# Twelve row one-hot slots in place of eight, and the mix's product, sum and spill taken up later in the step loop of a graph layer

## What is computed

```python
xn = layernorm(x)                              # x: 6250 x 256, f32
# two graph layers over 200,000 edges (src, dst); src uniform, dst = 6250 * u**2 with u uniform
agg = segment_sum(h[dst], src); h = silu(norm((h + agg / deg) @ W.T + b) * g + beta)
# a linear attention mix, 8 heads of 64: dots = k.T v (k, v normalised), out = q dots / N
mix = (q @ dots / N) @ w_out.T + b_out
x = x + gnn(xn) + mix
x = x + moe_ffn(layernorm(x))                  # 2 of 8 experts, layer norm after
```

## Time and profile before

| | |
|---|---|
| median of 3 runs | 3315.58 us (3312.92 to 3317.39) |
| profiled execution, its own time | 3316.68 us |
| its span, first to last instruction | 3314.9 us |
| step loop in it | about 666 to 1742 us |
| PE busy | 2628.7 us (79%) |
| DVE busy | 2009.6 us (61%) |
| ACT busy | 1309.2 us (39%) |
| mean granted PE clock | 0.924 of full speed |

### The profile page before, as it was taken

The page is one execution under the profiler, slowest core; times in us unless marked ns, Lnnn a source line. Parts: engine busy times, 40 slices in busy tenths (PEclk is TensorE's granted clock), DMA queues, the critical chain, the costliest instruction groups (busy, mean ns, idle before and its releaser), DMA issues. The chain is left out here.

```text
span 3314.9 us, 54424 instructions
## 1 busy us (share of the span) xinstructions
PE 2628.7 (79%) x16782; PEld 1850.4 (56%) x16782; DVE 2009.6 (61%) x4822; ACT 1309.2 (39%) x2213; POOL 169.5 (5%) x160
## 2 busy tenths in 40 slices
PE   0666555575858888877768999999799999986997
PEld 0333343332324444443327888888688888864665
DVE  8878899989888888889961222222122222236555
ACT  0333212244646666667691222222222221225666
POOL 0000000000000000000000000000011111114000
PEclk9888768687989999999969999999899999997999
DMA  5000000013213223223324444444544444410000
GB/s 159 0 0 1 0 0 0 10 45 132 104 56 127 104 91 117 98 95 121 121 81 155 150 148 150 143 147 151 182 137 138 138 130 137 138 60 29 26 25 27
DMA packets 153846, 304.75 MB, mean 92 GB/s; under 512 B 28963, under 2 KB 125476, under 8 KB 153700
## 3 DMA queue, kind: packets, MB, share of 16 engines
q1 hardware_dynamic: 101796, 217.44, 20.7%
q10 hardware_dynamic: 51776, 85.24, 7.0%
q0 software_dynamic: 128, 0.26, 0.0%
HBM read 196.54 MB, written 106.37 MB: 91 GB/s over the span
## 5 line engine op out<-in xcount | busy, mean ns | idle before, releaser
L1046 PE MATMUL banks<-ring 128*128 128x512 f16 x1650 | 517.2, 425 | 256.7 <-DVE ring L1652 126.8
L1076 PE MATMUL banks<-outer,ring 128*128 128x257 f16 x2450 | 543.9, 274 | 15.6 <-DMA outer<-table,heavy 8.6
L743 ACT ACTIVATE ring<-banks 128x512 f16<-128x512 f32 x637 | 382.2, 600 | 433.3 <-POOLq L604 431.4
L1076 PE MATMUL banks<-tabs,ring 128*128 128x257 f16 x2450 | 542.4, 274 | 8.6 <-DMA ring<-counts 8.6
L1077 PE MATMUL banks<-outer,ring 128*128 128x256 f16 x2450 | 543.7, 273 | 0.0
L1077 PE MATMUL banks<-tabs,ring 128*128 128x256 f16 x2450 | 542.3, 273 | 0.0
L1652 DVE TENSOR_SCALAR ring<-val,outer 128x512 f16<-128x512 f16 x1650 | 473.4, 348 | 78.5 <-PE banks L1046 77.4
L1046 PEld LDWEIGHTS banks<-ring 128*128 128x128 f16 x1650 | 230.7, 146 | 512.8 <-issue 450.9
L744 ACT ACTIVATE banks<-banks 128x512 f32<-128x512 f32 x637 | 383.5, 602 | 0.0
L1076 PEld LDWEIGHTS banks<-outer,ring 128*128 128x128 f16 x2450 | 238.7, 97 | 49.0 <-DMA outer<-table,heavy 8.9
L1076 PEld LDWEIGHTS banks<-tabs,ring 128*128 128x128 f16 x2450 | 238.4, 97 | 41.9 <-issue 9.5
(11 more groups left out here) (337 smaller groups left out, 3012.2 us busy)
## 6 DMA issues: line engine op xcount, KB each, us to landing
ring<-counts SPq DMA_DIRECT2D x98, 800.0 KB, 4.7
counts<-ring ACTq DMA_DIRECT2D x84, 896.0 KB, 3.9
ring<-counts SPq DMA_DIRECT2D x98, 768.0 KB, 4.1
tabs<-in_fw SPq DMA_DIRECT2D x4, 2048.0 KB, 9.0
outer<-in_x SPq DMA_DIRECT2D x5, 1280.0 KB, 13.4
outer<-in_x SPq DMA_DIRECT2D x25, 256.0 KB, 2.8
residual<-outer SPq DMA_DIRECT2D x25, 256.0 KB, 2.1
table<-tabs SPq DMA_DIRECT2D x25, 256.0 KB, 2.5
```

The lines of the kernel that those rows point to most:

```text
L743: act.activation(held[:, b, :, c, :], cell_bank.rearrange("p (q r) -> p q r", r=P), ACT.Copy, scale=0.25).then_inc(s_cell, 1)
L1046: mm(ps[:, bass.ds(at, 512)], hot_c[:, t // 8 % 2, :, t % 8], hot_r[t % RSLOTS], start=False, stop=False, skip_group_check=True).then_inc( ...
L1076: mm(o[:, 0:D + 1], a, xtab[l][:, cb, D:2 * D + 1], start=cb == 0, stop=False)
```

## The change

- `RSLOTS` goes from 8 to 12. The four new slots lie in unused columns of `outer` (one) and `big` (three). The wait ahead of a group becomes "all but the last eight steps done".
- The output product is issued one tile at a time: tile 0 behind group n + 6, tile 1 behind n + 7, each with its own `s_op`. The copy to `xT` stands ahead of group n + 5, the sum ahead of n + 12, the spill ahead of gate n + 14, the x rows ahead of gate n + 18.
- The transposes of pair p wait for the copy of pair p - 1 (`s_oxT`); the sum of pair p - 1 is now waited for by the product.
- M and G products, their copies and the run facts stand six groups apart in place of four; `HEAVY_AT` 22 becomes 26, `WMAX_AT` 48 becomes 60, the first weight load is 26 groups behind `HEAVY_AT`, and `piece_rows` comes two groups later.

```diff
--- before.py
+++ after.py
@@ -59,7 +59,7 @@
 PB = [0, 128, 512, 1024, 1536, 2048, STEPS]
 CW = 7
 NBK = 4
-RSLOTS = 8
+RSLOTS = 12
 IOTA = 640
 
 assert W * P >= P * EC and RB <= 49 and G + 1 < 1 << 10 and NCB % CW == 0 and G < IOTA
@@ -90,7 +90,7 @@
 
 
 
-M_AT, HEAVY_AT, WMAX_AT, SCALES_AT = 2, 22, 48, 132
+M_AT, HEAVY_AT, WMAX_AT, SCALES_AT = 2, 26, 60, 132
 OUT_AT = {**{140 + 8 * i: i for i in range(10)}, **{260 + 8 * i: 10 + i for i in range(11)},
           **{388 + 8 * i: 21 + i for i in range(4)}}
 TABLE_AT = {424 + 5 * i: i for i in range(NP)}
@@ -99,10 +99,10 @@
 assert len(OUT_AT) == len(TABLE_AT) == NP and max(TABLE_AT) + 2 < NG
 
 
-SPILL_AT = {n + 9: p for n, p in OUT_AT.items()}
-XIN_AT = {n + 13: p + 2 for n, p in OUT_AT.items() if p + 2 < NP}
+SPILL_AT = {n + 14: p for n, p in OUT_AT.items()}
+XIN_AT = {n + 18: p + 2 for n, p in OUT_AT.items() if p + 2 < NP}
 WRITE_AT = {n + 2: p for n, p in TABLE_AT.items()}
-WLOAD_AT = {HEAVY_AT + 18: 0, **{WMAX_AT + 10 * k + 2: k + 1 for k in range(4)}}
+WLOAD_AT = {HEAVY_AT + 26: 0, **{WMAX_AT + 10 * k + 2: k + 1 for k in range(4)}}
 
 REST_AT = 200
 
@@ -247,6 +247,7 @@
         hot_c = ringf[:, 0:1024].bitcast(F16).rearrange("p (b c k) -> p b c k", b=2, k=8)
         hot_r = [ringf[:, 1024 + n * 256:1280 + n * 256].bitcast(F16) for n in range(6)]
         hot_r += [outer[:, 9152 + n * 256:9408 + n * 256].bitcast(F16) for n in range(2)]
+        hot_r += [outer[:, 12096:12352].bitcast(F16)] + [big[:, 3328 + n * 256:3584 + n * 256].bitcast(F16) for n in range(3)]
         held = ringf[:, 2560:6144].bitcast(F16).rearrange("p (b q c r) -> p b q c r", b=2, q=GR // P, r=P)
 
 
@@ -1008,17 +1009,18 @@
                     pe.wait_ge(s_sc, 3)
                     pe.wait_ge(s_w, 16 * 11)
                 else:
-                    pe.wait_ge(s_oa, p)
+                    pe.wait_ge(s_oxT, p)
                 transposes(xn[:, p * 2 * D:(p + 1) * 2 * D], bank[4]).then_inc(s_otp, 1)
 
-            def out_product(p):
-                pe.wait_ge(s_oxT, p + 1)
-                for q in range(2):
-                    for c in range(DC):
-                        mm(bank[6][:, q * D:(q + 1) * D], xT[p % 2][:, (q * DC + c) * P:(q * DC + c + 1) * P],
-                           g_s[:, c * D:(c + 1) * D], start=c == 0, stop=False)
-                    m = mm(bank[6][:, q * D:(q + 1) * D], ones[0:1, :], borow, start=False, stop=True)
-                m.then_inc(s_op, 1)
+            def out_product(p, q):
+                if q == 0:
+                    pe.wait_ge(s_oxT, p + 1)
+                    if p:
+                        pe.wait_ge(s_oa, p)
+                for c in range(DC):
+                    mm(bank[6][:, q * D:(q + 1) * D], xT[p % 2][:, (q * DC + c) * P:(q * DC + c + 1) * P],
+                       g_s[:, c * D:(c + 1) * D], start=c == 0, stop=False)
+                mm(bank[6][:, q * D:(q + 1) * D], ones[0:1, :], borow, start=False, stop=True).then_inc(s_op, 1)
 
             def banks_of_steps(at):
 
@@ -1052,18 +1054,19 @@
                             pe.wait_ge(s_ready, piece)
                             pe.wait_ge(s_oa, sum(o < n for o in OUT_AT))
                         piece_part(piece, n - first_n - 1)
-                if n in (M_AT, M_AT + 4):
-                    m_products((n - M_AT) // 4)
-                if n == M_AT + 8:
+                if n in (M_AT, M_AT + 6):
+                    m_products((n - M_AT) // 6)
+                if n == M_AT + 12:
                     g_products()
-                if n in (HEAVY_AT + 1, HEAVY_AT + 5, HEAVY_AT + 9, HEAVY_AT + 13):
-                    run_turn((n - HEAVY_AT) // 4)
+                if n in (HEAVY_AT + 1, HEAVY_AT + 7, HEAVY_AT + 13, HEAVY_AT + 19):
+                    run_turn((n - HEAVY_AT) // 6)
                 if n == SCALES_AT - 1:
                     weight_scales()
                 if n in OUT_AT:
                     out_transposes(OUT_AT[n])
-                if n - 4 in OUT_AT:
-                    out_product(OUT_AT[n - 4])
+                for q_out in range(2):
+                    if n - 6 - q_out in OUT_AT:
+                        out_product(OUT_AT[n - 6 - q_out], q_out)
             pe.wait_ge(s_free, NBK + G)
             pe.wait_ge(s_oa, NP)
 
@@ -1597,7 +1600,7 @@
                 dve.tensor_copy(xT[p % 2][:, :], bank[4]).then_inc(s_oxT, 1)
 
             def mixed(p):
-                dve.wait_ge(s_op, p + 1)
+                dve.wait_ge(s_op, 2 * p + 2)
                 dve.wait_ge(s_xin[p % 2], 16 * (p // 2 + 1))
                 dve.tensor_tensor(xin[p % 2], xin[p % 2], bank[6], op=ALU.add).then_inc(s_oa, 1)
 
@@ -1614,24 +1617,24 @@
                 for first_n, piece in PIECE_AT.items():
                     if 0 <= n - first_n <= CH:
                         chunks_past(piece, n - first_n)
-                    if n == first_n + CH + 5:
+                    if n == first_n + CH + 7:
                         piece_rows(piece)
                 if n == M_AT - 1:
                     dots_diagonal()
-                if n in (M_AT + 3, M_AT + 7):
-                    m_copy((n - M_AT) // 4)
-                if n == M_AT + 11:
+                if n in (M_AT + 5, M_AT + 11):
+                    m_copy((n - M_AT) // 6)
+                if n == M_AT + 17:
                     g_copy()
-                if n >= HEAVY_AT and (n - HEAVY_AT) % 4 == 0 and n <= HEAVY_AT + 16:
-                    runs((n - HEAVY_AT) // 4)
+                if n >= HEAVY_AT and (n - HEAVY_AT) % 6 == 0 and n <= HEAVY_AT + 24:
+                    runs((n - HEAVY_AT) // 6)
                 if n >= WMAX_AT and (n - WMAX_AT) % 10 == 0 and n < WMAX_AT + 40:
                     weights_max((n - WMAX_AT) // 10)
                 if n == SCALES_AT:
                     weight_scales()
-                if n - 3 in OUT_AT:
-                    mixed_xT(OUT_AT[n - 3])
-                if n - 7 in OUT_AT:
-                    mixed(OUT_AT[n - 7])
+                if n - 5 in OUT_AT:
+                    mixed_xT(OUT_AT[n - 5])
+                if n - 12 in OUT_AT:
+                    mixed(OUT_AT[n - 12])
                 if n in TABLE_AT:
                     table0(TABLE_AT[n])
```

## The result

The changed kernel takes **3258.61 us** (median of 4 runs, 3257.38 to 3263.99) against 3314.51 us of the kernel before (the three runs of the table above and a fourth): ratio 0.983, 95% interval 0.982 to 0.984. Its profiled execution has a span of 3255.6 us, against 3314.9. The forecast was 3245 us, in a range of 3224 to 3280. The kernel became faster by 56 us where 70 were forecast.

A forecast was written before the change was run, and what follows sets the result against it. The DVE was taken as the loop's main limit, with DVE, PE and ACT waiting in turn beside the mix output. Terms -49.1 + 6 - 9 - 6 - 8 - 4.4 = -70.5 us gave 3245 us, range 3224 to 3280.

The forecast's parts named there:

- The sum ahead of n + 7, -49.1 us: The DVE's wait for the mix's output product, 25 times, falls to zero with the sum ahead of n + 12: -49.1 us.
- Slots beside the mix, -9: DVE slot waits beside the mix output, 13.9 us, fall to 5: -9 us, bounds 0 and -13.9.
- ACT, +6: Six or seven row groups beside the mix output, bound by ACT in their last cells, charged 1 us each: +6.
- M and G products, -4.4: The DVE's waits for M and G products go, as it comes five groups behind them: -4.4 us.
- Pieces -6: DVE slot waits in three full pieces, where the PE is full: -2 us each, -6 in all, bounds -3 and -9.
- elsewhere -8: Slot waits beside run facts, maxima, scales and tables: 8 of some 22 us go, bounds -2 and -18.
- Place of the slots, SP, run facts, last stretch: 0: Slots in `big` cost nothing extra, SP keeps its lead, run facts aren't waited for, ACT limits the end: 0 each.
- Rival 1: PE and ACT take over, the mix period ends at 13.6 us: 3279 us, range 3265 to 3300; chance 0.23.
- Rival 2: Shorter dry spells keep the PE's clock up everywhere, nearly all slot waits go: 3221 us; chance 0.09.
- Rival 3: SP loses its lead at spills in light cells; at 3.4 us a pair the result is 3325 us; chance 0.03.
- Rival 4: The change does nothing, as ACT sets the row groups' length altogether: 3316 us; chance 0.03.
- The signs: If right: L1602 wait gone, slot waits about 60 us, period 12.3 to 12.7, layers some 70 us sooner, later stretches unchanged.

The follow-up runs named there:

- slots alone: The kernel before with twelve row slots in place of eight and nothing else: 3279.15 us, ratio 0.989.
- old spacing: The changed kernel with M, G, run facts, maxima, first weight load and piece rows back in their old places: 3260.66 us, ratio 0.983.

## Why the prediction was right, and where its sum was off

- *The sum ahead of n + 7, -49.1 us.* Right. The wait is zero, and slots alone don't remove it (55.0 us), as the order of queues said.
- *Slots beside the mix, -9, and ACT, +6.* This is the step that failed, in sign: slot waits there went from 15.7 to 34.4 us, +18.7. I compared the PE's and the DVE's work over eight groups, 11.3 against 12.0 us, and concluded that two products of 1.6 us are covered by a third group in hand. What counts is the time from the moment when the DVE has written group g to the moment when it gets g + 1 back done, against the three groups of one-hots that it can write meanwhile. In the rows above g is n + 6: from 1220.94 to 1225.01 it is 4.07 us, and the one-hots of n + 7 to n + 9 are done 3.75 us after 1220.94, so 0.32 us of waiting. Of the 4.07 us 0.92 + 1.59 + 0.92 are the PE's work; the other 0.64 are handing over, of which 0.34 pass ahead of the PE's first matmul. The expectations of the later runs had 0.3 us for this, by which no wait would be left behind n + 6. With 0.64 one sum gives the waits of all variants (in us; what wait is left is the first number less the second):

| variant | g, lump, g + 1 and handing over | one-hots in hand | wait by the sum | measured |
|---|---|---|---|---|
| one half, even g | 0.92 + 1.59 + 0.92 + 0.64 = 4.07 | 3.75 | 0.32 | 0.32 |
| both halves, even g | 0.92 + 3.27 + 0.92 + 0.64 = 5.75 | 3.75 | 2.00 | 2.01 |
| one half, even g, eight slots | 4.07 | 2.7 | 1.37 | 1.36 |
| one half, odd g, eight slots | 4.07 | 2.7 + 0.61 | 0.76 | 0.76 |
| one half, odd g | 4.07 | 4.4 | none | none in most periods |
| half without bias, even g | 0.92 + 0.86 + 0.92 + 0.64 = 3.34 | 3.75 | none | none in most periods |

Three groups behind an odd g hold two sets of column one-hots, so they take longer (4.4 us); with eight slots and an odd g one more set, 0.61 us, is written ahead of the wait. In the changed kernel the half behind n + 6 misses by 0.32 us, and the second one right behind n + 7 adds 0.76.

- The ACT charge, 6 us, can't be told apart: 5.2 to 9.8 us of slot waits are left in the mix groups without the product's part, mostly in the last cells of row groups. That ACT causes them is argued; no run here tested it.
- *M and G products, -4.4.* The waits are gone, the time isn't. The groups 0 to 18 took 39.22 us before and 39.21 after. The DVE waited 1.7 us for slots and 4.4 for M and G there, and now waits 6.1 for slots, 4.0 of it ahead of group 18: a piece is being multiplied in these groups, and the PE is full. The old spacing agrees, 3260.7 us.
- *Pieces -6, elsewhere -8.* The three full pieces with their rows (groups 97 to 125, 226 to 260, 354 to 388) became 4.9 us shorter, near the mark; elsewhere was too small. Outside the mix the loop gained 22.8 us in all, against 6 + 8 + 4.4 = 18.4 forecast; slots alone gave 25.7 there. So the wrong term for M and G was made up for, by luck and not by reasoning.
- *Place of the slots, SP, run facts, last stretch: 0.* Right: 346 ns in each place; SP's wait for sums fell from 37.5 us to 16.6, so its lead shrank but held; groups 533 to 550, the last row group, took 53.0 us before and 52.7 after.

```profile
SPq L477 <- DVE outer L1605: 16.6, 5, 6.8
```

- *Rival 1* said 13.6 us for a period, the forecast 12.3 to 12.7, and 13.27 was measured: its period was nearer, though its time (3279, from 3265) was not, and the PE was the engine, but by the order of its work and not by its sum, as with the same work the period came to 12.43 us. Its sign came about as well: new waits of 0.32 + 0.76 = 1.08 us a period behind the product. *Rival 2* fell: the groups that lay in 740 to 880 us became 2.5 us shorter, not 8. *Rival 3* too: the PE waited 94.4 us for gates in the loop, 99.3 before (its 3325 us should have read 3330, 3245 + 25 x 3.4). *Rival 4* is 56 us off. The rule of the Trainium skill (Perfetto Trace Analysis, Optimization Strategy), weighed in the prediction, that a repeated gap can mean too few buffers, was wrong for the largest gap and right for the loop: slots alone gave 37 of the 56 us, none of it at that gap.
- *The signs.* Of those named for the forecast two came about: the wait at the sum is gone, and nothing behind the loop changes length by more than 2 us. Three didn't: slot waits are 78.5 us and not 60, the period is 13.27 us, and the layers start 57.6 us sooner and not 70. All bounds of the terms taken at once give 3223 to 3271 us, wider than the 3228 to 3264 stated as the forecast's own.

So the sum: mix -33.3 and not -52.1, the rest -22.8 and not -18.4: -56 us and not -70.5. The larger error lies in the slot waits beside the mix, and a smaller one outside it of the other sign brought the total nearer.

## What to carry to other kernels

Two engines that hand over through a ring of k groups are not compared by their mean work. Take each lump of extra work on the consumer, add the groups on either side that the producer waits for and the time of handing over (0.64 us here, twice what was guessed), and hold that against what the producer needs for k groups; a lump that fits costs nothing, the part that doesn't is paid every time. Moving a wait's target further off and deepening the ring pay less one at a time than together where each uncovers the other: here 6 and 37 us alone, 56 together. And a wait that vanishes in a stretch where another engine is full comes back as another wait, so read the stretch's length and not the list of waits.

## What the runs showed of the hardware

The two bias matmuls of a half, one row deep and 256 columns wide in f32, are dear on the queue: without them a half takes 0.86 us and not 1.58, so 0.72 us for two matmuls with one row of operand, against 0.86 for the four that multiply with 128 rows. The weight loads (PEld) of the changed kernel stand idle for 0.33 us ahead of them and again ahead of the next one-hot step; without them the load of the next step (at 1202.90) begins within the product and shows no such gap.

```profile
1223.26 0.29 PEld L1023 LDWEIGHTS banks<-big,ones 1*128 1x128 f32 x2 [0.33 <-issue]
...
1223.88 0.64 PEld L1048 LDWEIGHTS banks<-ring 128*128 128x128 f16 x4 [0.33 <-issue]
```

```profile
1202.90 0.79 PEld L1048 LDWEIGHTS banks<-ring 128*128 128x128 f16 x4
```

Why the loads wait there isn't shown. The changed kernel without them is 34 us faster, 1.4 us for each of 25 pairs; 29 of the 34 us are slot waits of the DVE that are gone.
